# Edges of a two-layer graph network in blocks of 30 tiles whose node range follows the block, with node rows read back from DRAM

## The reference

```
layer 0   q, k, v = x Wq + bq, x Wk + bk, x Wv + bv          (8 heads of 32)
          score   = clip(q[dst] . k[src] / sqrt(32), -10, 10)
          alpha   = softmax of score over the edges of a dst
          y       = (sum over edges of alpha * v[src]) Wp + bp;  x0 = x + y
          out0    = x0 + gelu(LN(x0) W1 + b1) W2 + b2
x1 = LN(x + out0)
layer 1   z = leaky_relu((x1 Ws)[src] + (x1 Wt)[dst], 0.2);  e = z . w_attn
          alpha   = softmax of e over the edges of a *src*
          out1    = (sum over edges of a dst of alpha * x1[src]) Wfc + bfc
result = LN(x1 + out1)
```

## Time and profile before

| | us |
|---|---|
| median of 3 runs (4416.05 to 4426.93) | 4420.28 |
| the profiled execution | 4421.56 |
| its span, first to last instruction | 4419.7 |
| PE busy (share) | 2636.1 (60%) |
| DVE busy | 2387.9 (54%) |
| ACT busy | 1328.2 (30%) |
| POOL busy | 2389.6 (54%) |
| 708.07 MB moved, mean rate | 160 GB/s |

### The profile page before, as it was taken

The page is one execution under the profiler, slowest core; times in us unless marked ns, Lnnn a source line. Parts: engine busy times, 40 slices in busy tenths (PEclk is TensorE's granted clock), DMA queues, the critical chain, the costliest instruction groups (busy, mean ns, idle before and its releaser), DMA issues. The chain is left out here.

```text
span 4419.7 us, 59683 instructions
## 1 busy us (share of the span) xinstructions
PE 2636.1 (60%) x12270; PEld 1915.8 (43%) x12271; DVE 2387.9 (54%) x6515; ACT 1328.2 (30%) x3525; POOL 2389.6 (54%) x2340
## 2 busy tenths in 40 slices
PE   5666666666666666884333333333333695777776
PEld 2344444444444445663122222222222594656565
DVE  4555555555555553442444444444445665666665
ACT  0355555554555553331122222222222100111111
POOL 0455555555555552113666666666666474666664
PEclk9788878787887778987666666666666556988988
DMA  3555655555565553114666666666667104655655
GB/s 129 157 172 172 176 169 170 174 170 165 172 172 172 171 171 66 48 48 131 185 191 189 187 191 192 194 194 194 195 194 191 40 0 141 194 191 191 195 190 166
DMA packets 347135, 708.07 MB, mean 160 GB/s; under 512 B 81680, under 2 KB 217797, under 8 KB 347102
## 3 DMA queue, kind: packets, MB, share of 16 engines
q0 software_dynamic: 151200, 472.92, 37.6%
q1 hardware_dynamic: 188840, 223.45, 16.2%
q10 hardware_dynamic: 7062, 11.34, 0.7%
HBM read 625.16 MB, written 82.35 MB: 160 GB/s over the span
## 5 line engine op out<-in xcount | busy, mean ns | idle before, releaser
L747 PE MATMUL ps_px<-sb_parts,sb_bits 128*128 x5400 | 987.0, 345 | 1004.2 <-DVEq L1422 666.9
L619 POOL DMA_INDIRECT sb_ring<-kv_rows,sb_idx x900 | 883.8, 982 | 775.8 <-DVE sb_msg L1291 406.9
L747 PEld LDWEIGHTS ps_px<-sb_parts,sb_bits 128*128 128x128 bf16 x5400 | 635.1, 122 | 1372.1 <-DVEq L1422 613.3
L761 PE MATMUL ps_pa<-sb_msg,sb_onehot 128*128 128x264 f32 x1800 | 642.8, 491 | 391.0 <-DVE sb_msg L1291 345.0
L988 ACT ACTIVATE sb_bits<-sb_bits 128x256 bf16<-128x256 bf16 x900 | 361.2, 409 | 1051.5 <-remote 668.8
L1276 DVE TENSOR_TENSOR sb_prod<-ps_px,sb_ring 128x512 f32<-128x512 f32 x450 | 309.8, 688 | 648.9 <-remote 405.6
L761 PEld LDWEIGHTS ps_pa<-sb_msg,sb_onehot 128*128 128x128 f32 x1800 | 387.8, 239 | 531.8 <-DVE sb_msg L1291 367.4
L619 POOL DMA_INDIRECT sb_ring<-proj_rows,sb_idx x300 | 286.9, 956 | 270.3 <-DMA sb_idx<-in_src 100.9
L619 POOL DMA_INDIRECT sb_w<-narrow_rows,sb_idx x300 | 288.1, 960 | 169.9 <-DVEq L1422 87.6
L1425 DVE SCALAR_TENSOR_TENSOR sb_prod<-sb_msg,sb_attn_hi 128x256 f32<-128x256 f32 x900 | 334.3, 420 | 1.5 <-DVE sb_prod L1425 0.8
L1291 DVE TENSOR_TENSOR sb_msg<-sb_ring,sb_msg 128x512 f32<-128x512 f32 x450 | 308.3, 685 | 0.2 <-issue 0.2
(11 more groups left out here) (220 smaller groups left out, 3760.0 us busy)
## 6 DMA issues: line engine op xcount, KB each, us to landing
sb_bits<-dst_short SPq DMA_DIRECT2D x304, 192.0 KB
x_edges<-sb_ring SPq DMA_DIRECT2D x50, 768.0 KB
sb_slots<-x_edges SPq DMA_DIRECT2D x50, 768.0 KB
x_edges<-sb_slots SPq DMA_DIRECT2D x25, 768.0 KB
sb_w<-x_edges SPq DMA_DIRECT2D x25, 768.0 KB
sb_msg<-lo_rows SPq DMA_DIRECT2D x26, 576.0 KB
sb_ring<-kv_rows,sb_idx POOLq DMA_INDIRECT x900
kv_rows<-sb_slots ACTq DMA_DIRECT2D x25, 256.0 KB, 2.0
```

The costliest lines, as they stand in the source:

```text
L619: pool.indirect_dma_start(out=out[:, i, :], out_offset=None, in_=rows, in_offset=bass.IndirectOffsetOnAxis(ap=idx[:, 2 * p + i:2 * p + i + ...
L747: mm = pe.matmul(px[:, j, 0:width], onehot_t[:, j, :], flat(parts[:, bass.ds(w, 1), a, 0:width]), start=(a == 0), stop=(a == 2))
L761: mm = pe.matmul(pa[:, 0:C + H], onehot[:, j, :], msg[:, j, :], start=False, stop=True, skip_group_check=True)
```

## The change

- *Blocks.* A visit is now a block of G = 30 tiles (S = 10, so the K/V ring has five pairs), and 27 blocks cover the 806 tiles. The node range of a visit starts at the smallest destination of the block, n, and holds 128 nodes from there. The tables find the least and greatest destination of each block; if one spans more than WN = 125 nodes, or neighbours start more than 124 apart, the visits go by 25 windows of 125 nodes instead, as before.
- *Carried sums.* A node at a block's edge has edges in two blocks. In place of the factor `carried`, the sums of the earlier visit are moved to the new range by a matmul with a shifted one-hot (`shift_hot`), which PE adds to the open sums during the next visit (`sums_carried`, `agg_carried`). The zeroing matmul is dropped; the first sum of a visit starts the bank.
- *Node rows through DRAM.* As ranges overlap and start anywhere, `parts` no longer holds all nodes. The three bf16 parts are stored to `part_rows` batch by batch, and SP loads the 128 rows of a visit into one of two places one visit ahead. y goes to `y_rows` per visit and is loaded per batch. Destination ids have five buffers and load a visit ahead.
- *x1.* It is reloaded into `ring` after the second pass, no longer before it. Its rows for `output` are loaded per visit.
- *Second and third pass.* 16 of a visit's 30 tiles have wide rows, and are streamed in the third pass; 14 are narrow, and are gathered.
- *Denominators.* POOL's part goes to DVE, in one product over all three parts. Weights and streamed operand are exchanged (128x128 against 128x75), chunks hold 31 tiles, 806 matmuls in all; the separate step that added the three parts is a reduction on DVE.
- *Scaled rows and outputs.* The rows of `feat_rows` are scaled and stored in five pieces. The output is stored per visit, 125 rows from n.

```diff
-G = 36
-S = 12
+WN = N_NODES // W
+G = 30
+S = 10
+BLOCKS = -(-T // G)
+SPAN = 2 * R
+LOOKED = THIRDS * SPAN
+STREAM = (R, R, R - 2)
-DT = 26
+DT = 31
...
+        visit_parts = parts[:, NB:NB + 2]
-        bits = sb("bits", [P, 5, R, P], BF16)
-        drow = bits[:, 0:2].bitcast(I16)
+        bits = sb("bits", [P, HALVES + 3, R, P], BF16)
+        drow = bits[:, 0:HALVES].bitcast(I16)
-        prod = sb("prod", [P, 2, 2 * C])
+        prod = sb("prod", [P, 3, 2 * C])
+        def streamed(p):
+            return p // RING % 2 == 0 and p != PAIRS - 1
...
# SP, in an edge pass
+                def node_parts(node, parity):
+                    sp.dma_start(visit_parts[:, bass.ds(parity, 1), :, 0:width].rearrange("p o a c -> p (o a) c"),
+                                 part_rows[bass.ds(node, P), :, 0:width]).then_inc(node_in[L], 16)
+                def products_out(v):
+                    node = visit_value(sp, "node", v)
+                    sp.wait_ge(wp_act, v * 2 + 3)
+                    sp.wait_ge(y_stored, v * 16 + 1)
+                    sp.dma_start(y_rows[bass.ds(node, P), :], y_stage).then_inc(y_stored, 16)
...
                     for h in range(HALVES):
                         sp.wait_ge(far[L], v * HALVES + h + 2)
-                        if h + 2 < HALVES:
-                            rows(tile, h + 2)
-                        else:
-                            rows(after, h + 2 - HALVES)
+                        rows(after, h)
...
+                        if h == 0:
+                            sp.wait_ge(expd[L], v * PAIRS + RING)
+                            sp.wait_ge(node_in[L], v * 16 + 16)
+                            node_parts(node, parity)
+                        if L == 0 and h == 3 and earlier is not None:
+                            products_out(earlier)
...
-            sp.dma_start(x1, proj_rows[:, CW:ROW].rearrange("(w p) c -> p w c", p=P)).then_inc(x1_back, 16)
-            edge_pass(1)
...
+            second_pass()
+            sp.wait_ge(slots_free[1], total * PAIRS + PAIRS)
+            sp.dma_start(x1, proj_rows[:, CW:ROW].rearrange("(w p) c -> p w c", p=P)).then_inc(x1_back, 16)
...
# SP, third pass
+            def output_out(v):
+                node = visit_value(sp, "node", v)
+                sp.wait_ge(gv, v * GV + GV)
+                sp.wait_ge(out_stored, v * 16 + 1)
+                sp.dma_start(io["out"][bass.ds(node, WN), :], out_stage[0:WN, :]).then_inc(out_stored, 16)
...
# POOL
-            pool.wait_ge(dsplit, 5)
-            with pool.Fori(0, TD // DT // 2) as it:
-                for b in range(2):
-                    for a in range(2):
-                        pool.tensor_tensor(hi_ex[:, b, a * W:(a + 1) * W], hi_hot[:, b],
-                                           e_parts[:, a, bass.ds(t0, DT)]..., ALU.mult).then_inc(dx, 1)
...
# PE, first pass
+                if p == 0:
+                    pe.wait_ge(node_in[L], v * 16 + 16)
-                        mm = pe.matmul(px[:, j, 0:width], onehot_t[:, j, :], flat(parts[:, bass.ds(w, 1), a, 0:width]),
+                        mm = pe.matmul(px[:, j, 0:width], onehot_t[:, j, :], flat(visit_parts[:, bass.ds(parity, 1), a, 0:width]),
...
+            def sums_carried(v):
+                pe.wait_ge(nd, v * ND + NDS["shift"])
+                pe.matmul(pa[:, 0:C + H], shift_hot[:], agg[:], start=False, stop=True, skip_group_check=True)
...
# PE, denominators
-                        mm = pe.matmul(pn[0:3 * W, 0:P], hi_ex[:, b, :, j], lo_hot[:, b, :, j],
+                        mm = pe.matmul(pn[:, 0:3 * W], lo_hot[:, b, :, j], hi_ex[:, b, :, :, j].rearrange("p a n -> p (a n)"),
...
# PE, third pass
+            def agg_carried(v):
+                pe.wait_ge(dgs, v * len(DGS) + DGS["shift"])
+                pe.matmul(pa[:, 0:C], shift_hot[:], agg[:, 0:C], start=False, stop=True, skip_group_check=True)
...
# DVE
-                dve.scalar_tensor_tensor(out=agg[:], in0=agg[:], scalar=carried[:, bass.ds(v, 1)], in1=pa[:, 0:C + H],
-                                         op0=ALU.mult, op1=ALU.add).then_inc(nd, 1)
+                dve.tensor_copy(agg[:], pa[:, 0:C + H]).then_inc(nd, 1)
...
+                dve.tensor_scalar(shift_hot[:], iota[:], moved[:, bass.ds(v + 1, 1)], None, ALU.is_equal).then_inc(nd, 1)
...
-                    dve.tensor_tensor(hi_ex[:, b, 2 * W:3 * W], hi_hot[:, b],
-                                      e_parts[:, 2, bass.ds(t0, DT)].unsqueeze(1).broadcast_to([P, W, DT]), ALU.mult).then_inc(dv, 1)
+                    dve.tensor_tensor(hi_ex[:, b], hi_hot[:, b].unsqueeze(1).broadcast_to([P, 3, W, DT]),
+                                      e_parts[:, :, bass.ds(t0, DT)].unsqueeze(2).broadcast_to([P, 3, W, DT]), ALU.mult).then_inc(dv, 1)
...
-            dve.tensor_tensor(feats[:], x1, denom[:, 2].unsqueeze(2).broadcast_to([P, W, C]), ALU.mult).then_inc(fv, 1)
+            for i in range(NB):
+                some = slice(i * W // NB, (i + 1) * W // NB)
+                dve.tensor_tensor(feats[:, some, :], x1[:, some, :], denom[:, 2, some]..., ALU.mult).then_inc(fv, 1)
```

More of the change, by code:

```diff
@@ L487, in edge_pass @@
+                fetch, value = visit_registers(sp, f"sp{L}", "tile", "node", "parity")
                 fetch(0)
-                tile, _ = value()
-                for h in (0, 1):
+                tile, node, parity = value()
+                for h in range(HALVES):
                     rows(tile, h)
@@ L492, in edge_pass, with visit @@
                     indices(tile, c)
-                with sp.Fori(0, total) as v:
-                    tile, _ = value()
+                def visit(v, earlier=None):
+                    tile, _, _ = value()
                     fetch(v + 1)
-                    after, _ = value()
+                    after, node, parity = value()
                     for h in range(HALVES):
@@ L594, in _ @@
                 low_rows(after)
+                if earlier is not None:
+                    output_out(earlier)
+                    features(v)
+            visit(0)
+            with sp.Fori(0, total - 2) as u:
+                visit(sp.snap(u + 1), u)
+            output_out(visit_before(sp))
+            features(last_visit(sp))
             sp.wait_ge(lo_in, total * 16 + 16)
@@ L706, in _ @@
         def _(pe):
+            pe.wait_ge(tables, TABLES["blocks"])
+            pe.matmul(px[:, 2, 0:2 * NBLK], ones[0:NBLK, :], block_diag.rearrange("p a k -> p (a k)"), start=True, stop=True).then_inc(tab_pe, 1)
             pe.wait_ge(tables, TABLES["linked"])
@@ L932, in sums @@
                         pe.wait_ge(early_added, v + 1)
-                    if p == PAIRS // 2 and earlier is not None:
+                    if p == EARLY and earlier is not None:
                         pe.wait_ge(gv, earlier * GV + GVS["agg"])
@@ L1180, in _ @@
             n = 20
-            dve.wait_ge(span_red, 1)
-            end, start = span_all[0:1, 0, :], span_all[0:1, 1, :]
             def link(ins):
@@ L1366, in first_norm @@
                 dve.wait_ge(npl, it * NPL + NPS["xm"] + 1)
-                rows = [flat(wide[:, bass.ds(it * NB + s, 1), 0:C]) for s in range(NB)]
+                rows = [y_batch[:, s] for s in range(NB)]
                 statistics(it, rows, 0)
```

540 lines of the change are left out of this document (330 added, 210 removed).

## The result

The changed kernel takes 4085.34 us (median of 4 runs, 4079.9 to 4093.65) against 4420.39 for the kernel before in the same comparison: ratio 0.9242, 95% interval 0.9221 to 0.9264, 335 us less. The forecast was 3995 us, so 90 us of the expected gain did not come: the time lies outside the forecast's own range (3925 to 4060) and inside the wider one (3915 to 4130), which had been widened for rivals 1 and 2. The profiled execution took 4088.86 us, span 4087.0, mean granted clock 0.76.

What follows compares the result with a forecast made beforehand. The prediction took the edge passes to be paced by ring waits, with PE-to-reader delays scaling with pairs or gathers. Its terms summed to -426 from the profiled 4421.6 us, giving 3995 us; own range 3925 to 4060, widened to 3915 to 4130.

Steps and rivals of the forecast that it cites:

- Rival 1: Second and third pass: bytes pace them, so -70 and -21 in place of -137 and -56, 4097 us; chance 0.17.
- Rival 2: Denominators: weights bound the matmuls, +116 in place of -84, 4195 us, or unchanged cadence, 4067 us; chance 0.16.
- scales with pairs or gathers: All three edge passes: the microsecond delay between PE and its readers was taken to grow with pairs or gathers.
- the third pass: Third pass with outputs: 48 us first interval, then 26 visits of 23.4 us, -56 us, bounds -80 and -15.
- 405 x 3.11 = 1260: Second pass: 405 pairs at the old 3.11 us a pair, plus 4 us for two boundaries, -137 us.
- The paragraph on the end: End of the third pass: outputs stored per visit leave only the last one standing alone, about 2.5 us; -10 us.
- First pass: First edge pass: 405 pairs at 3.45 us, plus visit boundaries and a smaller ring, 1406 against 1551 us, -145.
- The ring's small term (+5): First pass: shrinking the row ring from 6 pairs to 5 costs +5 us, as gathers hardly ever release a product.
- Denominators: Denominators: POOL leaves and operands swap, the stream pays for the stride, 114 against 198 us, -84.
- The small terms: Tables and projections +9, batches +7, start of the second pass -18, x1 reload's new place +8, end -10 us.
- Rival 4: All edge passes: blocks are not taken, so 50 visits and 750 pairs, about 6760 us; chance 0.01.

Runs made afterwards that it cites:

- e11: Changed kernel with first-pass messages ahead of the product, narrow second-pass gathers and half of each streamed row in the third: passes 1403.7, 1286.7 and 688.1 us.
- e12: Changed kernel with K alone gathered (first pass), POOL at most six pairs ahead (second), low rows earlier and outputs later in SP's queue (third): 1360.6, 1217.3, 655.5 us.
- e13: Changed kernel with first-pass messages ahead of the product, POOL at most six pairs ahead, and SP's third-pass loads and stores reordered: 3955.48 us, ratio 0.9086.
- e6: Changed kernel with only the denominators' operand exchange undone, sums unused: its 806 matmuls take 177.5 us against 112.4 with the exchange.

## Why the prediction was right, and where it was not

*What bounds the kernel.* The delay between PE and its readers was seen and named. It is what the traces of the two conditions differ in, in just the three passes that differ, 4352 to 4420 against 3695 us in all for one kernel; what brings it about is open. That it "scales with pairs or gathers" fits the first pass: POOL's time over its issue went from 16.7 us a visit of 18 pairs to 14.4 of 15, and 3.45 us a pair gave 3.456. It is wrong for the second. That the total still fell into the stated range is in part luck: the range had been widened for two rivals whose mechanisms did not occur (4085 lies above the 4060 of the forecast alone), and the third pass came at -7 outside its own bounds of -80 and -15.

*Second pass, the step that failed.* "405 x 3.11 = 1260" took a mean over visits for a cost per pair. DVE's row sums have 1.34 us between them at the median; the mean is made by pauses. In a steady visit POOL's first gathers stand 55.6 us apart before, 45.5 us of issue and 10.1 over it, and 48.2 after, 37.8 and 10.4. The part over the issues did not shrink with the pairs. Shrunk by 15/18 it would be 8.4: 2.0 us less in each of 26 visits, 52 us, where 51 are missing. The pauses got fewer and longer: 3.2 a visit of 3.2 us before, nearly all ended by a freed place, and 2.4 of 4.3 us after, of which the one ahead of the visit's first gather is ended by SP's load of the indices. Why their sum stayed is not shown; the order of SP's queue in this pass was not varied. Rival 1 named a time for this pass, -70, that lies nearer to the -86, and by the prediction's own sign 3.25 us a pair is nearer to bytes (3.3) than to the forecast (3.11); but e11 rules that mechanism out, and so the equal rates of 190 and 192 GB/s in two kernels were a result of the pauses, not their cause.

*Third pass, the step that failed.* 23.4 us a visit were forecast, and (4073.3 - 3410.5)/26 = 25.5 came, 54 us more in 26 visits; the first interval took 42.5 where 48 were forecast and gave 5 back. The paragraph on the end had the reason and dismissed it: SP waits in each visit for the earlier output, "the next indices are queued behind it, and POOL waits for those, but the output is done by the middle of the visit". Two views of the changed kernel show the contrary: the waits of the third pass (engine, tile and line waited for, us in total, times, longest), and the order of SP, DVE and POOL in one visit.

```profile
DVE sb_bits L1720 <- DMA sb_msg<-lo_rows: 44.2, 15, 4.0
POOL sb_w L757 <- DMA sb_idx<-in_src: 41.4, 6, 8.0
```
```profile
3622.66 0.33 SPq L667 DMA_DIRECT2D sb_w<-x_edges  x1
3623.84 0.26 SPq L671 DMA_DIRECT2D sb_msg<-lo_rows  x1
3624.56 0.98 POOL L757 DMA_INDIRECT sb_wqkv<-feat_rows,sb_idx  x1 [0.30 <-issue]
3626.26 0.35 SPq L687 DMA_DIRECT2D out<-sb_hn  x1
3627.76 0.35 SPq L679 DMA_DIRECT2D sb_tr<-proj_rows  x1
3629.29 0.33 SPq L675 DMA_DIRECT2D sb_idx<-in_src  x1
3629.54 0.82 DVE L1720 TENSOR_SCALAR sb_bits<-sb_msg,sb_hn 128x2304 bf16<-128x2304 bf16 x1 [3.02 <-DMA sb_msg<-lo_rows]
3631.83 1.05 POOL L757 DMA_INDIRECT sb_w<-feat_rows,sb_idx  x1 [6.29 <-DMA sb_idx<-in_src]
```

POOL had issued its last gather at 3624.56 and stood until 3631.83, behind a 0.33 us load that SP issued after an output it had waited for. Moving the two took 43 us off (e12, e13), of the 49 missing. In the prompt condition moving them gained nothing (536.0 against 532.7 us): a queue order that is free in one condition is a new wait in the other. That the late semaphores are what delays SP is inferred from this pair; it was not measured by itself.

*First pass.* -153 for -145. The ring's small term (+5) holds in the late condition alone: the rows land about 6 us ahead of their product before and about 3 after (medians over the landing events that are recorded), so the smaller ring ate slack. In the prompt condition the slack is 0.1 us in both, and the ring took back about 88 us (405 x (2.84 - 2.62)).

*Denominators.* -81 for -84, and e6 shows that the streamed side sets the pace. That it does so by its stride rests on the prediction's comparison with contiguous operands; no run removes the stride. DVE is level with PE, as forecast at 4.0 us a chunk: it is busy 106.6 us in the stretch, 4.1 a chunk, PE's 31 matmuls at 0.133 us are 4.1 too, and PE waits for DVE 26 times. Rival 2 is out by e6. The Trainium skill, "TensorE: Matmul & The Clock Gate", section "Weight-path perf modes — Fast Weight Load (FWL) and DoubleRow", has fast loads for 128 columns that are not fp32, packed or strided. The trace agrees so far as the strided 128-column loads kept up with a matmul every 0.133 us. Their records last 143 ns against 208 for 75 columns, but in each kernel a load's record is about as long as the step between matmuls (0.133 and 0.220 us), so what a load costs by itself is not shown.

*The small terms* (tables, batches, start, reload, end) came within 4 us each. The reload's wait is DVE's 6.87 us ahead of the iota copy. Rival 4 is out by the counts of 405.

## What to carry to other kernels

Take a mean per item apart into the engine's own cadence and its pauses before scaling it to another count: what recurs per visit need not shrink with the items in a visit. When a step is added to an in-order queue, price what is queued behind it by the latest time at which its wait can end, not by the middle of the visit. And an engine that may run far ahead is not free: holding POOL at six pairs ahead instead of fifteen took 75 us off the second pass in the condition in which semaphores came late (e12, e13), with nothing else changed in that pass.

## What the runs showed of the hardware

- The same kernels ran in two conditions, 3685 to 3707 and 4346 to 4367 us for the kernel before (4416 to 4427 in the first timing). Stages without gathers are the same within 2.5 us (denominators 187.9 and 187.9, tables 149.2 and 146.9 in the kernel before); the three passes of either kernel take 20 to 32% longer in the late one. What puts a run into one or the other is open.
- In the late condition PE's recorded semaphore events come after the last modelled end of the matmuls they tell of by 1.7, 2.5 and 0.01 us (medians) and up to 6.7, 16.5 and 7.3 us in the first, second and third pass of the changed kernel; in its tables, batches and denominators, where nothing is gathered, by 0.01 us, as in the passes of the prompt condition. The first pass's events of DVE and ACT, as far as recorded, stand 0.01 us behind their instructions in both conditions (one of ACT's 0.22).
- In the three passes of the late condition events of PE, DVE and ACT are missing from the trace: 337 of 405 are recorded for the second pass's expansions and 196 of 405 for the message products that free the K/V ring, against 404 and 405 in the prompt condition. In the batches and denominators none is missing.
- Of DVE's 82 waits over 2 us in the changed kernel's second pass 56 end 1.3 to 4.7 us (median 2.5) after the end of POOL's last gather issue, the rest closer to an issue or during one. The size of the rows hardly matters (1024 bytes a row less in 432 gathers: 0.5%); a smaller lead of POOL helps (6%). Whether the events wait on their path, or PE's matmuls end later than their modelled ends, is not shown by any run.
- Matmuls with both operands at a stride of 62 bytes start 0.220 us apart with 128 columns streamed on 75-column weights, at a granted clock of 0.50 (1.2 GHz), and 0.133 us apart with the operands exchanged.
